# A graph layer's neighbour sums split into two column tiles: 18 full-width steps become 11 rounds of two 64-node halves, in two bursts

## What is computed

```
z = layernorm(x)
agg   = segment_sum(z[src], dst)                     # over all edges
neigh = agg / max(degree, 1)
h = z @ W_self + b_self + neigh @ W_neigh
h = layernorm(h) * gamma + beta
h = where(h >= 0, h, alpha * h) + z
x = x + h
g = layernorm(x)
x = x + (silu(g @ q(w_gate).T) * (g @ q(w_up).T)) @ q(w_down).T   # 512 -> 1408 -> 512, weights ternary per group of 128
```

## Time and profile before

| quantity | value |
|---|---|
| median of 3 runs | 1694.86 us (1693.52 to 1698.13) |
| profiled execution, first to last instruction (span) | 1674.1 us |
| median less the span, outside the instructions | 20.8 us |
| PE busy | 1537.9 us, 92% |
| ACT busy | 1177.1 us, 70% |
| DVE busy | 1055.9 us, 63% |
| POOL busy | 938.3 us, 56% |
| gathers | 882, 231.27 MB |

### The profile page before, as it was taken

The page is one execution under the profiler, slowest core; times in us unless marked ns, Lnnn a source line. Parts: engine busy times, 40 slices in busy tenths (PEclk is TensorE's granted clock), DMA queues, the critical chain, the costliest instruction groups (busy, mean ns, idle before and its releaser), DMA issues.

```text
span 1674.1 us, 21796 instructions
## 1 busy us (share of the span) xinstructions
PE 1537.9 (92%) x6421; PEld 750.7 (45%) x6422; DVE 1055.9 (63%) x2305; ACT 1177.1 (70%) x2248; POOL 938.3 (56%) x936
## 2 busy tenths in 40 slices
PE   7999989987889999999999998999998998989897
PEld 3444434444444454444444444444444443444343
DVE  8999624655565565564665756557466466573876
ACT  5577500026777787778787786869887887879796
POOL 2123277666676666666666766667666666764000
PEclk9999989989998999999999999999999999999999
DMA  9869488997776887777777867787777777784101
GB/s 303 257 219 292 125 293 313 274 282 208 213 226 189 225 224 221 218 229 210 216 212 226 228 201 230 209 235 211 217 209 223 218 213 223 206 228 129 38 14 37
DMA packets 210883, 353.40 MB, mean 211 GB/s; under 512 B 105482, under 2 KB 105482, under 8 KB 210754
## 3 DMA queue, kind: packets, MB, share of 16 engines
q0 software_dynamic: 70560, 231.27, 47.4%
q1 hardware_dynamic: 140204, 120.73, 24.5%
HBM read 295.79 MB, written 39.62 MB: 200 GB/s over the span
## 4 chain that ended last, share of the span: by engine, by line
PE 84%; issue 6%; ACT 6%; DVE 2%; DMA 1%; another core or an unknown queue 0%; DVEq 0%; SPq 0%; ACTq 0%
PE f_ps L994 21%; PE f_ps L995 20%; PE f_ps L807 20%; PE agg_ps L889 10%; PE agg_ps L891 10%; ACT f_ps L1088 4%; PE side_ps L934 1%; PE agg_ps L803 1%; PE side_ps L803 1%; PE f_ps L889 0%; PE f_ps L891 0%; ACT hT L1113 0%; ACT acc L1098 0%; DVE acc L1440 0%; DMA rows<-in_x 0%
## 5 line engine op out<-in xcount | busy, mean ns | idle before, releaser
L759 POOL DMA_INDIRECT rows<-node_table,idx x882 | 891.6, 1011 | 442.6 <-issue 241.3
L1088 ACT ACTIVATE f_ps<-f_ps,ratio 128x512 f32<-128x512 f32 (+2 forms) x1303 | 777.0, 666 | 240.6 <-PE f_ps L995 163.2
L994 PE MATMUL f_ps<-x1T,tern 128*128 128x512 f16 (+2 forms) x1144 | 424.2, 374 | 52.0 <-issue 28.2
L995 PE MATMUL f_ps<-x1T,tern 128*128 128x512 f16 (+2 forms) x1144 | 422.4, 372 | 0.0
L889 PE MATMUL agg_ps<-rows,hot 128*128 128x512 f16 x846 | 328.5, 388 | 22.8 <-issue 22.8
L891 PE MATMUL agg_ps<-rows,hot 128*128 128x512 f16 x846 | 326.1, 385 | 4.3 <-issue 4.3
L1440 DVE SCALAR_TENSOR_TENSOR acc<-f_ps,scl,acc 128x512 f32<-128x512 f32 (+2 forms) x143 | 102.4, 717 | 229.0 <-PE f_ps L995 116.4
L994 PE MATMUL f_ps<-hT,tern 128*128 128x512 f16 (+2 forms) x572 | 213.4, 376 | 25.6 <-issue 13.0
L995 PE MATMUL f_ps<-hT,tern 128*128 128x512 f16 (+2 forms) x572 | 212.6, 374 | 0.0
L994 PEld LDWEIGHTS f_ps<-x1T,tern 128*128 128x128 f16 x1144 | 113.1, 99 | 216.6 <-issue 67.2
L889 PEld LDWEIGHTS agg_ps<-rows,hot 128*128 128x128 f16 x846 | 120.1, 142 | 133.3 <-issue 64.2
(11 more groups left out here) (176 smaller groups left out, 1705.1 us busy)
## 6 DMA issues: line engine op xcount, KB each, us to landing
rows<-node_table,idx POOLq DMA_INDIRECT x882
hsx<-own_rows SPq DMA_DIRECT2D x49, 256.0 KB
hsx<-in_x SPq DMA_DIRECT2D x48, 256.0 KB
out_nodes<-work SPq DMA_DIRECT2D x48, 256.0 KB, 2.2
xj<-xnt_rows SPq DMA_DIRECT2D x26, 256.0 KB
node_table<-work SPq DMA_DIRECT2D x25, 256.0 KB, 3.1
acc<-own_rows SPq DMA_DIRECT2D x23, 256.0 KB
own_rows<-acc SPq DMA_DIRECT2D x23, 256.0 KB
```

The costliest lines, as they stand in the source:

```text
L759: pool.indirect_dma_start(out=rows[:, j, :], out_offset=None, in_=table[:, :], in_offset=bass.IndirectOffsetOnAxis(ap=of[:, j:j + 1], axis ...
L994: pe.matmul(to, lhs, parts[0], start=g == 0, stop=False, skip_group_check=True)
L995: pe.matmul(to, lhs, parts[1], start=False, stop=True, skip_group_check=True).then_inc(p_ff, 1)
L1088: act.activation(ps, ps, ACT.Copy, scale=ratio[:, w if up else 2, j:j + 1]).then_inc(a_scaled, 1)
```

## The change

The 128 nodes of a block are split into two halves of 64. The edges are sorted by target, so the lower half's edges lie in the first tiles and the upper half's in the last. The lower half takes tiles 0 to 9 and the upper half tiles 7 to 17; tiles 7, 8 and 9 are read by both. There are 11 rounds. In a round each half has one tile: its matmul has 64 weight columns and writes 64 partitions of `agg_ps`, and the two halves' matmuls stand next to each other in the instruction stream. Per block that is 42 matmuls of 512 columns: 11 rounds, two parts, two halves, less the one that has no tile in round 0. They run in two bursts, rounds 0 to 5 at the end of tick 8 and rounds 6 to 10 at the end of tick 17.

```
+    def tile_of(h, i):
+        return STRIDE * h - 1 + i          # STRIDE = 8
+    BURST_ROUNDS = [range(0, 6), range(6, ROUNDS)]
+    BURST_AT = {8: 0, TICKS - 1: 1}
+    SHARED = [7, 8, 9]
...
-            def sum_step(b, j):
+            def sum_burst(b, n):
+                pe.wait_ge(v_hot, b + 1)
+                if n == 0:
+                    after(pe, v_h0, b)
+                pe.wait_ge(gathered[len(BURST_ROUNDS) * (b % 2) + n], 16 * ARRIVE[n] * (b // 2 + 1))
+                for i in BURST_ROUNDS[n]:
+                    for part in range(2):
+                        for h in range(HALVES):
+                            if tile_of(h, i) < 0:
+                                continue
+                            lo = h * HN
+                            mm = pe.matmul(agg_ps[lo:lo + HN, :], hot[:, b % 2, i, lo:lo + HN],
+                                           rows[:, row_at(b, tile_of(h, i)), part * D:(part + 1) * D],
+                                           start=(part == 0 and i == (0 if h else 1)),
+                                           stop=(part == 1 and i == ROUNDS - 1), skip_group_check=True)
+                mm.then_inc(p_used, 1)
```

More of the change, by code:

```diff
@@ L166, in norm_tick, with row_at, freed_by, used_all @@
         return 7 if t < BLOCKS + 1 else 4
-    AGG_AT = [[] for _ in range(TICKS)]
-    for j in range(STEPS):
-        AGG_AT[2 + j * (TICKS - 2) // STEPS].append(j)
+    def tile_of(h, i):
[3 more added lines that the diff above has]
+    SHARED = [7, 8, 9]
+    ORDER = []
+    for i in range(ROUNDS):
+        ORDER += [j for j in (tile_of(1, i), tile_of(0, i)) if j >= 0 and j not in ORDER]
+    assert sorted(ORDER) == list(range(STEPS))
+    SINGLE = [j for j in ORDER if j not in SHARED]
+    assert all(tile_of(h, i) in SHARED for h in range(HALVES) for i in range(ROUNDS)
+               if (h, i) in ((1, 0), (1, 1), (1, 2), (0, 8), (0, 9), (0, 10)))
+    BURST_OF = {j: next(n for n, rounds in enumerate(BURST_ROUNDS) if i in rounds)
+                for h in range(HALVES) for i in range(ROUNDS) for j in [tile_of(h, i)]}
+    for j in SHARED:
+        BURST_OF[j] = len(BURST_ROUNDS) - 1
+    FIRST_USE = {j: min(n for n, rounds in enumerate(BURST_ROUNDS) if any(tile_of(h, i) == j for h in range(HALVES) for i in rounds))
+                 for j in range(STEPS)}
+    ARRIVE = [sum(n == FIRST_USE[j] for j in ORDER) for n in range(len(BURST_ROUNDS))]
+    def row_at(b, j):
+        if j in SHARED:
+            return SINGLE_RING + len(SHARED) * (b % 2) + j - SHARED[0]
+        return (b * len(SINGLE) + SINGLE.index(j)) % SINGLE_RING
+    def freed_by(b, j):
+        if j in SHARED:
+            return used_all(b - 1)
+        before = b * len(SINGLE) + SINGLE.index(j) - SINGLE_RING
+        if before < 0:
+            return 0
+        return used_all(before // len(SINGLE)) + BURST_OF[SINGLE[before % len(SINGLE)]] + 1
+    def used_all(blocks):
+        return len(BURST_ROUNDS) * blocks
     def is_last(kind, g):
@@ L592, in overflow @@
                             end = sp.value_load(rangei[0:1, bass.ds(b + BLOCKS, 1)], min_val=0, max_val=E)
-                            with sp.Fori(first, end, PASS) as at:
+                            with sp.Fori(first, end, OPASS) as at:
                                 n = sp.snap(passes)
@@ L755, in _, with gather @@
                 pool.wait_ge(st_xt[i], 16 * len(range(i, len(LATER), XTR)))
-            def gather_load(of, load, s):
-                for j in range(load * PER_LOAD, (load + 1) * PER_LOAD):
-                    pool.indirect_dma_start(
-                        out=rows[:, j, :], out_offset=None, in_=table[:, :],
-                        in_offset=bass.IndirectOffsetOnAxis(ap=of[:, j:j + 1], axis=0)).then_inc(s, 16)
+            def gather(at, of, s):
+                pool.indirect_dma_start(
+                    out=rows[:, at, :], out_offset=None, in_=table[:, :],
+                    in_offset=bass.IndirectOffsetOnAxis(ap=of, axis=0)).then_inc(s, 16)
             def overflow():
@@ L786, in _ @@
             for b in range(BLOCKS):
-                pool.wait_ge(ld_idx[b % 2], 16 * (b // 2 + 1))
-                for load in range(LOADS):
-                    after(pool, p_used, (b - 1) * LOADS + load + 1 if b else 0)
-                    gather_load(idx[:, b % 2], load, gathered[load])
+                pool.wait_ge(v_idx, 2 * b + 2)
+                for j in ORDER:
+                    after(pool, p_used, freed_by(b, j))
+                    gather(row_at(b, j), idx[:, b % 4, j:j + 1], gathered[len(BURST_ROUNDS) * (b % 2) + FIRST_USE[j]])
         @block_ctx.tensor
@@ L808, in product, with turned_out, turn_edges @@
                                  skip_group_check=True)
+            def turned_out(t):
+                return sum(at < (t, 0) for at in TURN_AT)
+            def turn_edges(b):
+                pe.wait_ge(ld_edges[b % 2], 32 * (b // 2 + 1))
+                if b == 2:
+                    pe.wait_ge(v_inv, 1)
+                if b >= 2:
+                    after(pe, v_out, turned_out(b - 2))
+                    pe.wait_ge(v_idx, 2 * b)
+                pe.transpose(edge_bank(b), edges[:, b % 2, :], identf[:, :]).then_inc(p_edges, 1)
             turn0(0)
@@ L1300, in count_edges @@
                 after(dve, p_deg, b)
-                for lo, hi in ((0, 44), (44, 88), (88, P)):
-                    with nc.allow_low_precision(reason="whole numbers up to STEPS"):
-                        dve.tensor_reduce(degs[:, lo:hi], hot[:, b % 2, lo:hi, :], AX.X, ALU.add).then_inc(v_degs, 1)
-                    yield
+                with nc.allow_low_precision(reason="whole numbers up to ROUNDS"):
+                    dve.tensor_reduce(degs[:, :], hot[:, b % 2].rearrange("p i m -> p m i"), AX.X, ALU.add).then_inc(v_degs, 1)
             for b in range(2):
```

391 lines of the change are left out of this document (213 added, 178 removed).

## The result

The changed kernel takes 1825.08 us (median of 3 runs, 1812.78 to 1839.61) against 1694.86, a ratio of 1.0762 with a 95% interval of 1.0678 to 1.0846. It is slower, by 130 us, where 1613 us was forecast.

The account below looks back on a forecast made before the run. PE, 84% of the chain that ended last, was taken as the bound. Terms -110 + 26 + 5 - 3 = -82 us on a span of 1674.1 gave 1592; with 20.8 us carried, 1613 us, range 1545 to 1680.

Parts of the forecast that it names:

- rival A: Sum on PE: the halves run in line, 42 x 0.216 us a block, giving 1798 us; chance 0.12.
- rival B: Sum on PE: weight loads are not hidden, 6.3 us a block, giving 1661 us; chance 0.12.
- The drain at a shape change: PE going in and out of two bursts: a 0.164 us tail exposed four times, 0.66 us a slot, ends 0 and 1.23.
- PE's content: Second stage, PE's work per slot: 24.5 us before, less a balance of 2.25 us from the change.
- The step that failed: Second stage: mean slot falls from 27.0 to 25.3 us and stays above POOL's 23.5.
- rival C: Second stage: shape change is free and POOL binds at 23.5 us a slot, about 1555 us; chance 0.18.
- The pace: ACT in slots of 42 or 39 steps takes longer than PE: 35 us excess, three quarters counted, +26 us.
- rival D: Light slots leave PE waiting for x1T, 4 us more at 11 chunks, 44 us, about 1660 us; chance 0.12.
- From span to median: Whole run: the median lies 20.8 us above the span, carried over unchanged.
- First stage: PE is full there, so 55 small matmuls count at least 0.100 us each: +5 us, ends 0 and 10.
- Tail: Slots 49 to 55 hold 227 steps in place of 233: -3 us.
- DVE: Count 1.7 us and one-hot 0.8 to 1.7 us a block; DVE gets no busier: 0, up to 0.5 us a slot if late.

Follow-up runs that it names:

- experiment 8: Changed kernel with the old pace and the burst's loops turned, all matmuls of one half before the other's; 1614.17 us, a single timing.
- experiment 1: Changed kernel with the planner's old pace, 38 and 35 steps a slot in place of 42 and 39; 1521.18 us, ratio 1.0001.
- experiment 4: Changed kernel with its 11 rounds spread one at a time over the slot and the old pace, 38 and 35; 1569.70 us, ratio 1.0326.
- 3: Changed kernel with its 11 rounds spread one at a time over the slot, new pace 42 and 39 kept; 1621.18 us, ratio 1.0670.
- experiment 5: Changed kernel again without an edit, where the kernel before takes 1519.11 us; 1559.33 us, ratio 1.0258.
- experiment 7: Changed kernel with the old pace and 3 of 18 gathers a block left out from the third block on (part of the sum missing); 1504.50 us, 0.9895.
- experiment 10: Changed kernel with the old pace and one in eight of ACT's scalings given to DVE; 1760.73 us, ratio 1.0387 where the kernel before took 1698.71.
- experiment 2: Kernel before with only the new pace, 42 and 39 steps a slot in place of 38 and 35; 1565.36 us, ratio 1.0291.
- experiment 9: Changed kernel, pace 42, a chunk's first step due 25.2 ticks in place of 19.2 after its last block; 1851.51 us, ratio 1.0872.
- experiment 6: Kernel before without an edit, run for its profile beside the other experiments; 1522.32 us, a single timing.
- experiments 13 to 18: 13: changed kernel, 1.0274; 14, 17: with old pace, 1.0025, 1.0041; 16: also 15 of 18 gathers, 0.9944; 15, 18: kernel before, new pace, 1.0318, 1.0276.

## Why the prediction was wrong

**What held.** The halves run side by side (rival A, that they run in line, fell; experiment 8 shows what it would have cost). A burst's matmuls hide their weight loads, so rival B fell too: 22 places at 0.216. But the reason given against rival B was wrong, and that it fell was luck: two loads of 0.100 were to fit one after the other under a place, and the loads last

```profile
L987 PEld LDWEIGHTS agg_ps<-rows,hot 128*64 128x64 f16 x2058 | 125.9, 119 | 178.8 <-issue 105.6
```

0.12 us, so that two of them, 0.24, would not fit. The loads of the two halves overlap too. In experiment 1 the 20 loads of the second burst, of 0.11 us each, take 1.87 us, where one after the other they would take 2.2:

```profile
823.29 1.87 PEld L987 LDWEIGHTS agg_ps<-rows,hot 128*64 128x64 f16 x20 [0.76 <-issue]
```

The Trainium skill's rule that matmuls in different column groups run at the same time ("TensorE: Matmul & The Clock Gate", Part 3) holds here, at full overlap and not at the 79% worked out from its figures. The drain at a shape change was predicted at 0.66 us a slot with an end at 0; it is 0.4. The Trainium skill's other rule is that a change of mode drains the engine ("TensorEngine Tiling (Array Packing)", Key Properties). The trace shows that a change costs something, 0.09 us in and 0.09 out, but not that PE empties: the next matmul starts after 0.31 us, before the recorded end of the last one at 0.38. Spreading the rounds, with up to 18 more changes in a slot, costs 48 us (4 against 1) and 62 us (3 against 5); at 0.09 to 0.12 each they lift PE's content by some 2 us, from 22.2 to past POOL's 24.0, and the slot of experiment 4 is 600 / (438 / 18) = 24.7 us. PE's content came out at 22.2 us a slot where 22.25 was said.

**The step that failed** is the line "The predicted mean slot, 27.0 - (110 - 26) / 49 = 25.3 us, stays above 23.5". It takes PE's content off the slot one for one and carries the 2.7 us of "waits, drains and slower clock" over unchanged. The measured mean slot is 1451.5 / 49 = 29.6 us here and 24.1 us, unchanged, in experiment 1. Three things were wrong in it.

1. *The 2.7 us were not slack that a smaller PE content sits on top of.* On a 1520 chip the kernel before has none of them (PE 598.34 of 600 us), and POOL's need is 24.0 us against a slot of 24.1 to 24.3. There PE's 2.6 us come to nothing: experiment 1 is 1.0001. This is rival C's mechanism, POOL as the bound, with a floor of 24.0 where I had 23.5, and with a slot already at it. It is not the whole of it: with the floor taken away (experiment 7) 12 to 17 us come back. With bursts PE also waits between steps, 1.2 us a slot, mostly for ACT, where the kernel before has none. The prediction had such waits only as the excess of slots with 42 steps; they are there at pace 38 too. The prediction's own rows could have warned: 24.5 and 23.5 us of content in two engines leave 1.0 us to gain and not 2.25, unless the 2.7 us stay on top of whichever engine leads.

2. *On a 1695 chip the waits grew, from 2.7 to 7.8 us a slot.* The trace shows PE's signals coming up to 6 us late there. What each late signal costs depends on how much work stands between PE and ACT: six banks, 2.6 us of steps at 0.432. Before, at least one pair of matmuls of the sum, which need nothing of ACT, stood between the steps of each of 16 ticks; after, PE has steps alone for eight or nine ticks, runs six ahead and stops at each late signal (953.58 to 954.32 above). Experiment 10 supports it: with the old pace the late starts between steps are 3.3 us a slot, where the kernel before has 1.4. That the bursts' layout makes the difference is still argued from these rows and not shown: experiment 10 also moved scalings to DVE, and no run had the sum spread on a 1695 chip.

3. *The pace was priced too low, and by the trace through the wrong mechanism.* The prediction gave it +26 us for ACT at its limit in slots of 42 steps. Its price is 38 us on the 1520 chips (1559.33 against 1521.18, 1562.69 against 1524.33) and 46 in the kernel before, and what the waits show beside it is rival D: PE stands before a chunk's first step. One such wait of the changed kernel, on the 1695 chip, and what it does to the clock:

```profile
905.30 0.38 PE L1088 MATMUL f_ps<-x1T,tern 128*128 128x512 f16 x1 [4.08 <-DMA x1T<-hsx]
905.52 0.38 PE L1089 MATMUL f_ps<-x1T,tern 128*128 128x512 f16 x1
905.74 0.58 PE L1088 MATMUL f_ps<-x1T,tern 128*128 128x512 f16 x1
906.11 0.63 PE L1089 MATMUL f_ps<-x1T,tern 128*128 128x512 f16 x1
906.53 0.63 PE L1088 MATMUL f_ps<-hT,tern 128*128 128x512 f16 x1
906.96 0.63 PE L1089 MATMUL f_ps<-hT,tern 128*128 128x512 f16 x1
```

After 4.08 us of waiting PE starts three matmuls 0.22 us apart and the following ones 0.42 to 0.43 us apart, at a granted clock of 0.50 from 906 to 909 us, which is the 1.2 GHz level. Rival D said 4 us at 11 chunks, 44 us; over the whole span of experiment 5 the row `PE f_ps L1088 <- DMA x1T<-hsx` holds 44.6 us in 11 waits (in experiment 2, 32.5 us in 12). That these waits are the price is argued from their size and from ACT's unchanged row: experiment 9, which was to take them away, ran on a 1695 chip. I gave rival D 0.12 and put it on a slot that still gained; it needed to be added to rival C, and the two together (nothing gained, 38 lost) match the 1520 chips.

**Smaller terms.** From span to median: 20.8 us were carried as time outside the instructions. It is 1.8 us in the profiled execution after and 2.4 to 2.9 in the 13 timings of the kernel before beside experiment 9. So the profile before is of an execution of some 1677 us (an estimate, 1674.1 and 2.5), faster than any of that kernel's timings on the 1695 chips (1688 and up), and the two spans are 7 us further apart than the two medians. First stage: +5 (0 to 10) predicted, +6.8 us measured (first gather at 215.6 against 208.8). Tail: -3 predicted; 0 on the 1695 chip, and with the new pace +7 us on a 1520 chip (137.9 us after the last gather in experiment 5, 130.8 in experiment 6). DVE: the count was taken at 1.7 us and the one-hot at 0.8 to 1.7; they are

```profile
L1391 DVE TENSOR_REDUCE degs<-hot 128x128 f16<-128x1408 f16 x49 | 124.5, 2541 | 0.0
...
L1382 DVE TENSOR_TENSOR hot<-dstl,node_j 128x1408 f16<-128x1408 f16 x49 | 79.2, 1617 | 0.0
```

2.54 and 1.62 us, together 4.16 where it was 4.2, so DVE gained nothing from 1408 numbers in place of 2304, and cost nothing either. Gathers and transfers: 0 predicted for the transfers and seen (DMA share 0.84 in experiment 1, 0.85 in 6).

**What stays open.** Why PE's signals are late on some chips: they go with the gathers (1% late in the tail, fewer with 15 gathers), DVE's and ACT's recorded ones are never late, but no run made or cured the lateness by itself. Nor is it shown that it is the chip and not the time or what else ran beside: each place was used in one comparison, and the record names no chip for the first one. And how the 7.6% split: on a 1695 chip 3.9% were left with pace 38 and ACT relieved, which suggests that layout and pace share it (the late starts of 3.3 us a slot, with either pace, speak for the layout), but neither the pace alone nor the tiles alone was measured on such a chip; experiments 13 to 18 were meant for it and fell on 1520 chips.

## What to carry to other kernels

Before a gain on the leading engine is subtracted from the period, work out every other engine's floor with its gaps (here 1.03 us busy and 0.30 us before each of 18 gathers) and ask what the "waits" of the profile are made of: a remainder that no engine's content explains can go with the place of the run, and is then not slack of the kernel. Measure a layout change apart from the schedule change that comes with it; here the layout cut PE's content as it was meant to, without a gain in time, and the pace lost 2.6%. Where two engines hand work back and forth through a few banks, independent work dealt between the steps covers the waits (0.0 us a slot before, 1.2 with bursts) and may be what covers late signals too, so bursts should be priced with that cover gone.

## What the runs showed that I had not expected

- Two 64-column matmuls with 512 moving columns each, next to each other in the stream, start 3 to 7 ns apart and a sustained run of pairs has a period of 0.216 us: double rate, and the two halves' weight loads overlap as well.
- PE pairs them across a short distance only: with ten of one half before twelve of the other, four overlapped.
- The cost of going into and out of column tiles is 0.09 us each, less than the 0.164 us by which a matmul's recorded length exceeds its place.
- A reduction of 1408 16-bit numbers a partition into 128 took 2.54 us, 1.8 ns a number, where one of 792 into 44 took 0.97 us, 1.2 ns a number.
- The same kernel takes 12% longer in some places (1695 to 1699 against 1519 to 1521 us), with PE's recorded signals up to several microseconds late, and only in the stage with gathers.
